# A three-term attention kernel: the folded table copied by ScalarE, the weight remainders made by GpSimd

## The reference

```python
h = relu(conv1d(embedding[ids], conv_w))          # context 2, grouped
h = h + attention(layernorm(h), Wq, Wk, Wv, Wo)   # 8 heads of 64, softmax over 1024 keys
h = h + ffn(layernorm(h))                         # fc1, gelu, fc2, one expert per 128 tokens, next_w, gelu
```

## Time and profile before

| what | value |
|---|---|
| median of three runs | 392.33 us |
| the profiled execution's own time | 392.45 us |
| its span in the profile | 390.4 us |
| busy: TensorE, VectorE, ScalarE, GpSimd | 379.4, 270.1, 273.3, 293.1 us |

### The profile page before, as it was taken

How to read it: one execution, slowest core, us unless ns; L and a number is a source line. 1 busy time by engine, 2 the same in 40 slices (tenths; PEclk the granted TensorE clock), 3 DMA queues, 4 the chain that set the end, 5 groups by cost and what they waited for, 6 DMA issues and landing times.

```text
span 390.4 us, 6725 instructions
## 1 busy us (share of the span) xinstructions
PE 379.4 (97%) x2382; PEld 222.4 (57%) x2382; DVE 270.1 (69%) x476; ACT 273.3 (70%) x388; POOL 293.1 (75%) x145
## 2 busy tenths in 40 slices
PE   8999999999999999999999999999999998999996
PEld 7756545554464455445545544555447444489995
DVE  6998677777868786777768777868775664665222
ACT  3666656678958886896888688868972787337753
POOL 3080476969999999999999999999999597700021
PEclk9999999999999999999999999999999999999999
DMA  4001002101212021103111331241024105000001
GB/s 141 12 0 40 15 3 57 54 3 55 58 54 55 3 56 56 56 10 82 20 56 52 77 98 50 57 162 57 3 57 164 54 3 162 0 2 15 14 29 54
DMA packets 28228, 19.45 MB, mean 50 GB/s; under 512 B 21248, under 2 KB 23680, under 8 KB 28196
## 3 DMA queue, kind: packets, MB, share of 16 engines
q1 hardware_dynamic: 27620, 18.05, 16.7%
q10 hardware_dynamic: 576, 0.98, 0.8%
HBM read 17.72 MB, written 1.17 MB: 48 GB/s over the span
## 4 chain that ended last, share of the span: by engine, by line
PE 90%; DVE 5%; ACT 2%; issue 2%; DVEq 0%
PE psum L669 29%; PE psum L658 24%; PE psum L596 11%; PE psum L584 5%; PE psum L605 4%; PE psum L726 4%; PE psum L715 4%; PE psum L560 3%; PE psum L680 2%; PE psum L535 1%; PE psum L621 1%; PE psum L623 1%; PE psum L734 1%; ACT probs L855 1%; PE psum L509 1%
## 5 line engine op out<-in xcount | busy, mean ns | idle before, releaser
L1088 DVE TENSOR_REDUCE half_maxes<-psum 128x1 f32<-128x512 f32 x232 | 149.0, 684 | 36.6 <-PE psum L596 35.8
L855 ACT ACTIVATE probs<-psum 128x1024 f32<-128x1024 f32 x128 | 124.7, 1022 | 60.3 <-PE psum L658 59.8
L669 PE MATMUL psum<-probs,v_all 128*64 128x512 f32 x512 | 123.7, 604 | 0.0
L1305 POOL TENSOR_TENSOR sums<-sums,probs 128x1024 f32<-128x1024 f32 x31 | 74.5, 2402 | 3.4 <-ACT probs L855 3.4
L1305 POOL TENSOR_TENSOR odd_sum<-odd_sum,probs 128x1024 f32<-128x1024 f32 x31 | 74.4, 2400 | 0.0
L669 PEld LDWEIGHTS psum<-probs,v_all 128*64 128x64 f32 x512 | 31.2, 136 | 62.8 <-issue 44.3
L1305 POOL TENSOR_TENSOR sums<-probs 128x1024 f32<-128x1024 f32 x16 | 38.1, 2379 | 31.0 <-ACT probs L855 31.0
L1133 DVE TENSOR_SCALAR psum<-max_plane 128x512 f32<-128x512 f32 (+1 forms) x50 | 40.5, 822 | 28.4 <-ACT probs L855 26.6
L596 PE MATMUL psum<-k_round,q_round 64*128 64x512 f32 x256 | 57.0, 446 | 2.0 <-DVE half_maxes L1088 1.1
L596 PEld LDWEIGHTS psum<-k_round,q_round 64*128 64x128 f32 x256 | 24.0, 183 | 53.9 <-DVE half_maxes L1088 41.4
L658 PE MATMUL psum<-q_round,k_round 64*128 64x512 f32 x256 | 52.4, 404 | 2.2 <-DVE psum L1133 2.2
(11 more groups left out here) (123 smaller groups left out, 451.3 us busy)
## 6 DMA issues: line engine op xcount, KB each, us to landing
max_plane<-rows_scratch SPq DMA_DIRECT2D x16, 512.0 KB, 3.7
inv_sb<-inv_scratch SPq DMA_DIRECT2D x14, 256.0 KB, 4.0
max_rows_of<-maxes SPq DMA_DIRECT2D x128, 0.5 KB, 2.0
v_all<-in_fc SPq DMA_DIRECT2D x4, 512.0 KB, 5.8
fc_late<-in_fc SPq DMA_DIRECT2D x4, 512.0 KB, 5.6
out_h<-probs SPq DMA_DIRECT2D x8, 128.0 KB, 1.8
v_all<-in_w ACTq DMA_DIRECT2D x3, 256.0 KB, 3.6
woT<-in_wo SPq DMA_DIRECT2D x1, 256.0 KB, 3.6
```

The costliest lines, as they stand in the source:

```text
L669: last = pe.matmul(out_bank[head_rows(h), :], v_all[:, s, kc, head_rows(h)], probs[unit(s, kc, half) % TILES][:, h, :], start=(kc == 0), s ...
L855: last = act.activation(probs[u % TILES][:, heads, :], source, ACT.Exp, scale=SCALE)
L1088: dve.reduce_max(half_maxes[:, h, qc, keys:keys + 1], slot[:, h, :], AX.X).then_inc(maxed, 1)
L1305: pool.tensor_tensor(chain[:, :, :], first[:, :, :], probs[kc][:, :, :], ALU.add).then_inc(own, 1)
```

## The change

ScalarE copies the folded table instead of VectorE. The copy stands in ScalarE's stream ahead of the wait for the weights' DMAs. The three weight remainders leave VectorE's stream and are made by GpSimd, after its constants and ahead of its wait for the second sequence's statistics.

```diff
@@ scalar
+            act.wait_ge(folded_ready, 1)
+            act.copy(folded[:, :], bank(3)[:, 0:TAPS * C]).then_inc(folded_sb, 1)
             act.wait_ge(w_loaded, 48)
             act.copy(wR[:, 1, :, :], raw_w[:, 1]).then_inc(weights_sb, 1)
             relu(0)
@@ vector
             make_onehot(1)
-            dve.wait_ge(folded_ready, 1)
-            dve.tensor_copy(folded[:, :], bank(3)[:, 0:TAPS * C]).then_inc(folded_sb, 1)
             make_onehot(2)
@@
-            def weight_rests(w):
-                dve.wait_ge(weights_sb, 2 - w)
-                dve.tensor_tensor(wL[:, w, :, :], raw_w[:, w],
-                                  wR[:, w, :, :].bitcast(F32), ALU.subtract).then_inc(w_rest, 1)
@@
-            weight_rests(1)
             x_statistics(0)
-            weight_rests(0)
             x_statistics(1)
             for g in range(NG // B):
                 x_inverse(g)
                 x_normalise(g)
-            dve.wait_ge(weights_sb, 3)
-            dve.tensor_tensor(wvL[:, :], raw_w[:, 2].rearrange("c r n -> c (r n)"), wvR[:, :].bitcast(F32), ALU.subtract).then_inc(wv_rest, 1)
@@ gpsimd
             last.then_inc(pads_made, 1)
+            for w in (1, 0):
+                pool.wait_ge(weights_sb, 2 - w)
+                pool.tensor_tensor(wL[:, w, :, :], raw_w[:, w], wR[:, w, :, :].bitcast(F32), ALU.subtract).then_inc(w_rest, 1)
+            pool.wait_ge(weights_sb, 3)
+            pool.tensor_tensor(wvL[:, :], raw_w[:, 2].rearrange("c r n -> c (r n)"), wvR[:, :].bitcast(F32), ALU.subtract).then_inc(wv_rest, 1)
             late = slice(KCH, 2 * KCH)
             pool.wait_ge(x_aggr, 2 * KCH)
```

## The result

The changed kernel takes 393.14 us (median of 20 runs, 392.48 to 393.70), the kernel before 392.45 us (median of 20 runs beside it; the three known at first had 392.33). One of these 20 runs of before, at 617.54 us, is a slow one and does not enter the ratio. The ratio is 1.0015, with a 95% interval from 1.0009 to 1.0022: slower by 0.35 to 0.86 us, and so within 0.2% or just past it. The forecast was 392.65 us; 393.14 us lies 0.04 us above its range.

What follows compares the result with a forecast made beforehand. TensorE, busy for 97% of the span, was taken as the bound. The copy's -0.68 us and the stall's +1.0 us gave +0.32 us on the 392.33 us median: 392.65 us, range 391.5 to 393.1 us.

Steps and rivals of the forecast that it cites:

- rows 9: Profile rows: a VectorE tensor_scalar at 2.80 ends 0.27 us after GpSimd's first memset; the second memset takes 0.27 us more.
- The stall's size: Normalisation on VectorE held up by GpSimd's value remainder: +1.0 us, bounds 0 and 1.29 us.
- 0.92 or 1.05: Stall in us if GpSimd gets in behind (0.92) or ahead of (1.05) the first normalisation group's fourth operation.
- at 12.42, it holds VectorE until 13.71: GpSimd's value remainder enters after the first normalisation group; the second group's first operation ends near 13.80, not 12.88.
- The copy's gain: Folded copy on ScalarE ahead of the convolution: convolution starts at 5.55 instead of 6.23, -0.68 us.
- The table's second product ends at 4.70 + 0.38 = 5.08: TensorE's table product, ahead of the folded copy: takes 0.38 us, so ScalarE can copy from 5.10.
- so I take 5.55: Convolution's start after the change, with TensorE busy spreading ids until 5.54; it stood at 6.23.
- The sum: Whole kernel: -0.68 us from the copy and +1.0 us from the stall, +0.32 us on the 392.33 us median.
- What was costed at nothing: Remainders leaving VectorE (2.0 us of its time), and key and query remainders running on GpSimd: 0 us.
- A: Rival: no collision at the normalisation, so only the copy's gain counts, 391.65 us; chance 0.32.
- B: Rival: GpSimd's value remainder into fp32r takes longer, 1.9 us, stall 1.6 us, result 393.25 us; chance 0.08.
- C: Rival: convolution does not move because one-hot or table is late, 392.3 us; chance 0.08 with an unforeseen ripple.

Runs made afterwards that it cites:

- e3: The changed kernel, with GpSimd's value remainder also waiting for the eight normalised chunks: 392.41 us against 392.34 for the kernel before.
- e6: The changed kernel, with ScalarE rounding the query weights ahead of the first relu and the value weights right behind it: 392.37 us against 392.36 before.
- e1: The kernel before with only the folded copy moved to ScalarE, all three remainders still on VectorE: 392.00 us against 392.34.
- e2: The changed kernel with the folded copy put back on VectorE, so only the three remainders move to GpSimd: 392.80 us against 392.34 before.
- e7: e2 with the value remainder back on VectorE and a GpSimd memset of an unread 128x1024 tile in its place: 392.89 us against 392.36 before.
- e8: e1 without TensorE's two spreads of the second sequence's ids, leaving out half of the convolution's input: 392.18 us against 392.36 before.
- e11: e1 with 5 TensorE warm-up products in place of 6: 392.53 us against 392.43 before.
- e5: The kernel before with only the key and query remainders moved to GpSimd; folded copy and value remainder stay on VectorE: 392.23 us against 392.36.
- e4: e2 with GpSimd making the value weights' subtraction twice in a row, first into an unread tile: 395.20 us against 392.34 before.

## Why the prediction was right and where it was off

**The sign and the mechanism.** The likeliest case was a gain at the copy, more than paid back by a stall of the normalisation behind GpSimd's value remainder. The stall is there in every trace with the overlap, and it goes when the overlap goes (e3, e6). The gain shows by itself in e1, though its interval holds no change; in the changed kernel it is not there. The Trainium skill (SBUF — State Buffer, Who interferes with whom) was cited against the change, and rows 9 were read as the same thing. The traces with the overlap agree, now also for the form with two per-partition operands: 0.75 us in the changed kernel and in e2, and 0.72 us behind an instruction that only writes (e7). The 13 traces also support the reading of rows 9: the `tensor_scalar` that starts at 2.80 there starts between 2.35 and 2.88 in them, and ends at 3.43 or 3.44 in all, 0.27 us after GpSimd's first memset.

**The stall's size.** The term was +1.0 us, worked out as 0.92 or 1.05. It measured 0.75. The step that was off is "at 12.42, it holds VectorE until 13.71": it let GpSimd in at the recorded end of the normalising operation. In e2 GpSimd's instruction shows 1.42 us, of which 1.28 are its own (1.27 to 1.28 in e3 and e6, 1.29 in the earlier trace rows), so by this estimate it waited 0.14 us and got in at 13.24, while the operation ahead of it ends only at 13.39 by its record. These are 0.15 of the 0.17 us by which 0.92 was too large; the rest lies in the lengths taken (1.29 for 1.28, and 0.09 for 0.08 us behind GpSimd's end).

**The copy's gain.** The term was -0.68 us. Only the lowest runs come near it: 391.66 us in e6 and 391.68 in e1, 0.7 us below the median of before, but 0.53 and 0.35 us below the lowest runs of before beside them; none of them has a trace. The median gain is 0.34 us in e1, and that is the most of the five kernels with the copy on ScalarE and no collision: by the medians e8 lies 0.18 us below its runs of before, and e6 lies 0.01, e3 0.07 and e11 0.10 us above them. Beside the moved remainders, in the changed kernel against e2, it is nothing by the medians. The steps that failed are "The table's second product ends at 4.70 + 0.38 = 5.08" and "so I take 5.55". They took TensorE's rate in one execution for the kernel's. The rate rises at another moment from execution to execution, and before the change VectorE's copy, which ends at 6.18, hid most of that. Taking the copy away uncovered it: the runs of the kernels with the copy on VectorE (e2, e5, e7) spread over 0.4 to 0.6 us, those with the copy on ScalarE (e1, e3, e6, e8, e11) over 0.8 to 1.3 us, in eleven runs each. In the profiled execution of the changed kernel the gain was even -0.23 us.

**The sum.** +0.32 was forecast, 0.59 by the ratio came out and 0.69 by the medians. The two halves had alone do not add up to it: -0.34 and +0.46 give +0.12. In spans they give -0.4 and +0.7, so +0.3, where the changed kernel has 391.0 for 390.4 (the profiled execution of before; the medians of its later runs are 390.3 or 390.4). Part of the difference lies outside the span (2.2 us in the changed kernel, 2.0 before, 1.8 in e2). The intervals of the halves (-0.59 to +0.08 and +0.20 to +0.90 us) are wide enough to hold the whole, so whether the copy gains less beside the moved remainders, and why, is open. That the total came near the forecast is in part luck: the gain was taken too large by 0.34 us or more, the stall by 0.25 us, and the two errors have opposite signs.

**What was costed at nothing** was right: the key and query remainders, taken off VectorE and put on GpSimd, make 392.23 for 392.36 (e5). The value remainder's leaving VectorE gains nothing either, since e3 and e6, without it and without the collision, are no faster than e1 (392.41 and 392.37 us for 392.00).

**The rivals.** A, no collision, is refuted by the profile. B, a longer subtraction into fp32r, as well: it takes 1.28 us where nothing is in its way (e3), like the sum into float32. C, a convolution that does not move, had been given little, and yet describes the profiled execution of the changed kernel, and by the times the changed kernel against e2. The table was late there, as C had it, and by the length of TensorE's products (631 for 378 ns), for which TensorE's rate is the reading.

**A version that beats both?** e1 lies 0.34 us below its runs of before and the changed kernel 0.69 us above its own, so e1 is about 1.0 us faster than the change by the medians, 0.8 us by the ratios. Against the kernel before its interval still holds 1: no version was found that is surely faster than that. e3 and e6 keep most of the change and are level with before.

## What to carry to other kernels

Work given to GpSimd was free here only where VectorE ran nothing beside it that a GpSimd instruction shuts out, as it does a `tensor_scalar` from SBUF to SBUF. Look not at GpSimd's slack, but at what VectorE does in the very microsecond in which the instruction will run; here a start 1.3 us later (e3) or 3.3 us earlier (e6) took the stall away. And measure the whole beside its halves: here the medians of the two halves gave 0.12 us and the whole 0.69. Before you price the removal of a link in the first microseconds, look at a second execution: TensorE's rate may rise at another time, and the link that you remove may be the one that hid it.

## What the runs showed of the hardware

- A VectorE `tensor_scalar` of 128x128 float32 with two per-partition operands, 340 ns alone, took 1090, 1091 and 1059 ns when a GpSimd instruction lay in its way, and ended 0.08 us after it each time. A memset by GpSimd, which reads nothing, did it too. Statistics (0.87 us for four) and their aggregation (0.36) kept their lengths beside GpSimd in e5, and so did the one-hots from PSUM in e2 (1.41 us for two, at 6.15, with GpSimd's subtraction from 6.55).
- Which engine goes first can't be read from the recorded starts to within 0.03 us: GpSimd's memset at 12.79 went ahead of an operation recorded at 12.76, its subtraction at 13.04 behind one that had started 0.06 us before. The two instructions differ, so the order may also hang on that.
- A copy of 128x256 from PSUM on ScalarE took 0.37 us, the value of the slope from its larger copies (373 ns).
- At the start TensorE's products take 631 ns in one execution and 378 in another for the same table product, while the granted clock column has 1.00 for both. In that stretch I go by the durations, not by the column. Later it agrees: at 0.50 in e4 a product of 128x512 took 0.63 us, at 1.00 it took 0.39.
- Two microseconds without work on TensorE (e4) were followed by a fall to 1.2 GHz that cost about another microsecond (e4's score product comes at 23.78 where e2's comes at 21.82, 1.96 us later, with 0.97 of it from the longer stall); 1.06 us (the changed kernel) were not.
